# Cross attention on one core: context and its weights split into high and low parts, keys and values made of three rounded products

## The chip, the cores and the metric

The kernel runs on one core of a Trainium2 chip. The metric is the device time of one execution in microseconds. A core has a matrix engine (TensorE, "PE" in the profile, with its weight loads as "PEld"), VectorE ("DVE"), ScalarE ("ACT"), GpSimd ("POOL") and SyncE ("SP"), which here only issues transfers. They work side by side and order each other by semaphores.

## What is computed

The reference is a cross attention of 20 heads of 32 channels with two sets of keys and values: the first 77 rows of the context ("text") and the other 77 ("image"), each with weights of its own. Cut to what matters:

```python
text = encoder_hidden_states[:, :77, :]      # (2, 77, 1024)
ip   = encoder_hidden_states[:, 77:, :]      # (2, 77, 1024)
q    = split_heads(hidden_states @ Wq.T)     # (2, 2048, 640) -> 20 heads of 32
k, v       = split_heads(text @ Wk.T), split_heads(text @ Wv.T)
k_ip, v_ip = split_heads(ip @ Wk_ip.T), split_heads(ip @ Wv_ip.T)
out = merge(attend(q, k, v)) + merge(attend(q, k_ip, v_ip))   # two softmaxes
return out @ Wo.T + bo + hidden_states
```

All arrays are float32.

## The kernel before

There are two stages: a prologue that makes keys and values, and a long loop over 80 units. A unit is one of 16 tiles of 256 query rows and one of 5 groups of 4 heads (128 channels).

**The prologue.** Four products of context and weights are made in this order: keys of text, keys of image, values of text, values of image. Each is `project_ctx` (L692 to 711): for each of the 8 chunks of 128 context channels (k) and each of the 5 groups of output channels (g), one matmul with a 128 x 128 block of the weights as the stationary operand and the context's chunk as the moving one (2 batches x 77 rows = 154 columns), in plain float32, added up in PSUM. That makes 40 matmuls a product, 160 in all. The weights of a product lie in `stage[br]`, 20 KB a partition, br being the branch (text 0, image 1); the context lies in `ctx`. Both arrive in five pieces, `PIECES`, of 1, 1, 2, 2 and 2 chunks, and TensorE waits for a piece (semaphores `ctx_loaded`, `wk_loaded`, `wv_loaded`) ahead of its first chunk. The value weights take the place of the key weights in `stage`, so SyncE (L244 to 256) sends for those of the text branch when the first product is done (`k_acc` at 1) and for those of the image branch when the second is (`k_acc` at 2). The query weights (1.6 MB) and the first tile of x go between the pieces of the text values.

Each engine's program is a list worked off in order. Around the prologue these are:

- ScalarE (L439 to 462): waits for `k_acc`, copies the keys out of PSUM in ten pieces (`keep_keys`), copies the query weights to their rounded high part (`weight_high`, L413), does the same for x (`split_x`), copies its half of the values of text out (`keep_v`), then begins with the first units.
- VectorE: subtracts the high part of the query weights from the raw ones (`weight_low`, L478 to 481), copies the other half of the values out (`keep_v`, L535), then the softmax of the first units.
- TensorE: a few warm-up matmuls (L729), the four products, and within the last of them the query projections of the first two units (`project_q`, 15 matmuls each) and the scores of these units, so that softmax work can start.

The end of the first use of the value banks is a hand-over: TensorE can't begin the fourth product before both halves of the third one's result are copied out (`v_kept`).

**Products of high and low parts.** The query and output projections are already made in another way: each float32 operand is split into a part rounded to the type `F32R` (the ScalarE copy) and the rest (raw less high, the VectorE or GpSimd subtraction, also `F32R`), and the product is the sum of three matmuls in `F32R`: high x high, low x high, high x low (`product_step`, L567 to 572). There the moving operand has 256 columns.

**The loop.** For each unit, TensorE does scores (L595), the query projection two units ahead (L571), the weighing of values (L623, L625), transposes of probabilities (L607, L615) and the output projection of six units before (L571); the other engines do the softmax. The change leaves the loop as it is.

## Time and profile before

| | us |
|---|---|
| time, median of 3 runs (lowest, highest) | 624.54 (622.1, 625.01) |
| the profiled execution's own time | 623.43 |
| its span in the profile | 621.4 |
| TensorE matmul busy, in the span | 599.5 |
| VectorE, ScalarE, GpSimd busy | 417.7, 338.6, 310.1 |

All rows come from one profiled execution. The span begins at its first instruction; times of day in the rows count from there. "Busy" of TensorE is the time with at least one matmul in flight: matmuls are pipelined, so the time from one start to the next (the pace) is shorter than the duration of one record. A pace is therefore read from a run of many records, not from their mean. The chain that ended last is followed back from the last instruction to what released each step; it tells what set the time. Idle time of an engine outside that chain costs nothing.

### The profile page before, as it was taken

The page shows a single profiled execution, that of the slowest core. Times are in us where ns is not written, and L with a number is a line of the kernel's source. Part 1 is how long each engine was busy: PE and PEld are TensorE (multiplying, and loading weights), DVE is VectorE, ACT ScalarE, POOL GpSimd, SP SyncE. Part 2 cuts the span into 40 slices and gives each one's busy share as a digit, 9 for nine tenths or more (in the row PEclk, how much of TensorE's full clock was granted, in tenths as well). Part 3 has the DMA queues.
Part 4 walks back from the last instruction along what each step waited for, and adds up shares of the span by engine and source line. Part 5 has one row for each costly group of instructions (what it writes and reads, how often), then busy time and mean ns, then how long its engine had stood idle before and what let it go on. Part 6 is the DMA issues. An engine that isn't in the chain of part 4 may idle for free.

```text
span 621.4 us, 14491 instructions
## 1 busy us (share of the span) xinstructions
PE 599.5 (96%) x5634; PEld 515.9 (83%) x5634; DVE 417.7 (67%) x496; ACT 338.6 (54%) x674; POOL 310.1 (50%) x341
## 2 busy tenths in 40 slices
PE   8999768999999999999999999999999999999986
PEld 8998557888888888888888888888888888888865
DVE  0035577777777777777777777777777777777761
ACT  0324554565666565656656565655656565565541
POOL 0033544465564746574655557465647555564550
PEclk9999888999999999999999999999999999999999
DMA  8980201112121212121121212121211112111001
GB/s 308 414 333 0 77 2 52 35 44 87 35 86 42 76 39 81 41 76 42 36 82 38 84 38 76 42 84 34 84 38 45 69 42 84 34 45 43 26 28 51
DMA packets 29402, 46.21 MB, mean 74 GB/s; under 512 B 3392, under 2 KB 24512, under 8 KB 29120
## 3 DMA queue, kind: packets, MB, share of 16 engines
q1 hardware_dynamic: 29376, 45.84, 21.5%
q8 instruction: 19, 0.31, 0.2%
q14 instruction: 7, 0.06, 0.0%
HBM read 35.34 MB, written 10.49 MB: 74 GB/s over the span
## 4 chain that ended last, share of the span: by engine, by line
PE 91%; ACT 4%; DVE 3%; DMA 1%; POOL 1%; SPq 0%; issue 0%; DVEq 0%
PE q_ps L571 24%; PE x_ps L571 21%; PE main_ps L607 11%; PE s_ps L595 9%; PE pv_ps L625 7%; PE pv_ps L623 7%; PE s_ps L707 3%; PE pv_ps L615 3%; PE pv_ps L707 2%; PE main_ps L707 1%; DVE row_max L489 1%; ACT probs L363 1%; ACT p_main L368 1%; DMA stage<-wk_in 1%; PE s_ps L658 1%; DVE wo_lo L481 1%
## 5 line engine op out<-in xcount | busy, mean ns | idle before, releaser
L306 POOL TENSOR_TENSOR probs<-probs,row_inv 128x616 f32<-128x616 f32 (+1 forms) x160 | 159.8, 1020 | 239.8 <-DVE row_inv L508 239.8
L489 DVE TENSOR_REDUCE row_max<-s_ps 128x16 f32<-128x1232 f32 x80 | 115.3, 1441 | 75.0 <-PE s_ps L595 75.0
L505 DVE TENSOR_REDUCE row_sum<-probs 128x16 f32<-128x1232 f32 x80 | 114.9, 1436 | 17.5 <-ACT probs L363 17.5
L497 DVE TENSOR_TENSOR probs<-s_ps,row_max 128x616 f32<-128x616 f32 x160 | 120.5, 794 | 2.7
L363 ACT ACTIVATE probs<-probs 128x616 f32<-128x616 f32 x160 | 114.2, 715 | 13.4 <-DVE probs L497 13.4
L358 ACT ACTIVATE q<-q_ps 128x256 f32<-128x256 f32 x80 | 30.6, 383 | 147.1 <-PE q_ps L571 147.1
L607 PE MATMUL main_ps<-ident,probs 128*122 128x128 f32 x640 | 96.6, 274 | 12.5 <-ACT p_main L368 9.1
L368 ACT ACTIVATE p_main<-main_ps 122x512 f32<-122x512 f32 x160 | 94.9, 593 | 15.5 <-PE main_ps L607 15.4
L607 PEld LDWEIGHTS main_ps<-ident,probs 128*122 128x122 f32 x640 | 75.6, 138 | 22.9 <-ACT p_main L368 10.5
L571 PE MATMUL q_ps<-x_hi,wq_hi 128*128 128x256 f32 x400 | 83.0, 306 | 0.0
L571 PE MATMUL x_ps<-attn_hi,wo_hi 128*128 128x256 f32 x375 | 75.2, 298 | 0.0
L571 PE MATMUL q_ps<-x_hi,wq_lo 128*128 128x256 f32 x400 | 74.5, 284 | 0.0
L571 PE MATMUL q_ps<-x_lo,wq_hi 128*128 128x256 f32 x400 | 74.1, 283 | 0.0
L512 DVE TENSOR_TENSOR attn_lo<-pv_ps,attn_hi 128x256 fp32r<-128x256 f32 x80 | 34.0, 425 | 57.5 <-ACT attn_hi L391 57.5
L571 PE MATMUL x_ps<-attn_lo,wo_hi 128*128 128x256 f32 x375 | 69.4, 283 | 0.0
L571 PEld LDWEIGHTS q_ps<-x_hi,wq_hi 128*128 128x128 f32 x400 | 58.6, 191 | 12.9 <-issue 12.6
L571 PE MATMUL x_ps<-attn_hi,wo_lo 128*128 128x256 f32 x375 | 69.1, 282 | 0.0
L297 POOL TENSOR_TENSOR x_lo<-x_raw,x_hi 128x1280 fp32r<-128x1280 f32 x16 | 48.9, 3055 | 37.6 <-ACT x_hi L380 37.6
L595 PE MATMUL s_ps<-keys,q 32*128 32x154 f32 x1280 | 65.7, 320 | 0.0
L386 ACT ACTIVATE y<-x_ps,bo 128x256 f32<-128x256 f32 x74 | 35.0, 473 | 53.9 <-PE x_ps L571 53.9
L571 PEld LDWEIGHTS q_ps<-x_hi,wq_lo 128*128 128x128 f32 x400 | 60.0, 192 | 0.0
L571 PEld LDWEIGHTS q_ps<-x_lo,wq_hi 128*128 128x128 f32 x400 | 59.3, 190 | 0.0
(71 smaller groups left out, 790.5 us busy)
## 6 DMA issues: line engine op xcount, KB each, us to landing
x_raw<-x_in SPq DMA_DIRECT2D x16, 640.0 KB, 3.8
res<-x_in SPq DMA_DIRECT2D x75, 128.0 KB, 2.0
y_out<-res SPq DMA_DIRECT2D x75, 128.0 KB, 1.7
stage<-wk_in SPq DMA_DIRECT2D x6, 640.0 KB, 8.2
stage<-wv_in SPq DMA_DIRECT2D x6, 640.0 KB, 10.7
wq_raw<-wq_in SPq DMA_DIRECT2D x1, 1600.0 KB, 11.2
wo_raw<-wo_in SPq DMA_DIRECT2D x1, 1600.0 KB, 7.4
stage<-wk_in SPq DMA_DIRECT2D x4, 320.0 KB, 5.7
```

What stands on the lines that cost most here:

```text
L297: nc.gpsimd.tensor_tensor(x_lo[:, u.batch], x_raw[:], x_hi[:, u.batch].bitcast(F32), ALU.subtract).then_inc(x_lo_done, 1)
L306: nc.gpsimd.tensor_tensor(rows[:, :, keys], rows[:, :, keys], row_inv[:, u.slot, :, br].unsqueeze(2) .broadcast_to([P, GROUP * SUB, size]) ...
L363: nc.scalar.activation(probs[:, u.slot, heads], probs[:, u.slot, heads], ACT.Exp).then_inc(exp_done, 1)
L368: nc.scalar.activation(p_main[0:MAIN, :, s * P:(s + 1) * P], main_ps[0:MAIN].rearrange("p (j n) -> p j n", j=GROUP), ACT.Copy).then_inc(ma ...
L489: nc.vector.tensor_reduce(row_max[:], by_row(s_ps[:, :, 0:SUB * BLK]), AXIS.X, ALU.max).then_inc(max_done, 1)
L497: nc.vector.tensor_tensor(by_row(probs[:, u.slot, heads].rearrange("p j s n -> p j (s n)")), by_row(s_ps[:, heads, 0:SUB * BLK]), row_max[ ...
L505: nc.vector.tensor_reduce(row_sum[:], by_row(probs[:, u.slot].rearrange("p j s n -> p j (s n)")), AXIS.X, ALU.add).then_inc(sum_done, 1)
L571: return nc.tensor.matmul(out, (lo if kind == 1 else hi)(k), (moving_lo if kind == 2 else moving_hi)(k), start=(n == 0), stop=(n == STEPS_ ...
L595: done = nc.tensor.matmul(s_ps[:, j, s * BLK:(s + 1) * BLK], q[rows_of(j), u.slot, s * P:(s + 1) * P], keys[rows_of(j), u.g, u.batch].rear ...
L607: done = nc.tensor.transpose(main_ps[0:MAIN, j * P:(j + 1) * P], probs[:, u.slot, j, s, 0:MAIN], ident[:])
L623: nc.tensor.matmul(pv_ps[rows_of(j), 0:N], v[:, u.g, u.batch, rows_of(j)], p_main[:, j, :], start=True, stop=False, skip_group_check=True)
L625: nc.tensor.matmul(pv_ps[:, 0:N], v[:, u.g, BATCHES + u.batch, :], p_rest[:], start=False, stop=True, skip_group_check=True).then_inc(pv_r ...
```

## The change

It touches the prologue only.

- New tiles: `stage_lo` and `ctx_lo` lie over `stage` and `ctx` (the low part is written over the raw data), `ctx_hi` is new, and `w_hi` is one buffer for the high parts of a whole product's weights, used by all four products in turn.
- ScalarE copies each piece of the context (keys' products only) and of the weights to its high part (`ctx_high`, `chunk_high`). From the second product on, a piece of `w_hi` may be written only when TensorE has used the same piece of the product before (`w_used`, and for the last piece `k_acc` or `v_acc`). The copies of keys, the split of the query weights and of x and the copy of the values are put between these copies in an order written out by hand.
- VectorE makes the low parts (`ctx_low`, `chunk_low`), with the low part of the query weights between those of the third product.
- TensorE waits for the low parts in place of the transfers, and makes three `F32R` matmuls with 154 moving columns in place of one in float32: 480 in place of 160.

```diff
@@ -144,8 +144,13 @@
         p_rest = sbuf("p_rest", [P, N])
 
         with ExitStack() as before:
-            stage = [sbuf(f"stage{i}", [P, CTX_CHUNKS * C], scope=before) for i in range(BRANCHES)]
-            ctx = sbuf("ctx", [P, BRANCHES, CTX_CHUNKS, BATCHES, KEYS], scope=before)
+            with ExitStack() as raw_before:
+                stage = [sbuf(f"stage{i}", [P, CTX_CHUNKS * C], scope=raw_before) for i in range(BRANCHES)]
+                ctx = sbuf("ctx", [P, BRANCHES, CTX_CHUNKS, BATCHES, KEYS], scope=raw_before)
+            stage_lo = [sbuf(f"stage_lo{i}", [P, CTX_CHUNKS * C], F32R, scope=before) for i in range(BRANCHES)]
+            ctx_lo = sbuf("ctx_lo", [P, BRANCHES, CTX_CHUNKS, BATCHES, KEYS], F32R, scope=before)
+            ctx_hi = sbuf("ctx_hi", [P, BRANCHES, CTX_CHUNKS, BATCHES, KEYS], F32R, scope=before)
+            w_hi = sbuf("w_hi", [P, CTX_CHUNKS, C], F32R, scope=before)
         attn_hi = sbuf("attn_hi", [P, BATCHES, GROUPS, N], F32R)
         attn_lo = sbuf("attn_lo", [P, BATCHES, GROUPS, N], F32R)
         res = sbuf("res", [P, GROUPS, N])
@@ -169,6 +174,9 @@
         wo_hi_done, wo_lo_done = sem("wo_hi_done"), sem("wo_lo_done")
         consts = sem("consts")
         head_rows_done = sem("head_rows_done")
+        ctx_hi_done, ctx_lo_done = sem("ctx_hi_done"), sem("ctx_lo_done")
+        w_hi_done, w_lo_done = sem("w_hi_done"), sem("w_lo_done")
+        w_used = sem("w_used")
         k_acc = sem("k_acc")
         k_done = sem("k_done")
         v_acc = sem("v_acc")
@@ -202,6 +210,17 @@
         v_banks = [pv_ps, main_ps]
         turn_banks = [x_ps, pv_ps, main_ps]
 
+        LAST_PIECE = len(PIECES) - 1
+
+        product_loaded = [*wk_loaded, *wv_loaded]
+        product_acc = [(k_acc, 1), (k_acc, 2), (v_acc, 1), (v_acc, 2)]
+
+        def piece_number(product, n):
+            return product * len(PIECES) + n + 1
+
+        def chunks_of(product, halves):
+            return halves[product % BRANCHES][:].rearrange("p (k c) -> p k c", k=CTX_CHUNKS)
+
         def rows_of(j):
             return slice(j * D, (j + 1) * D)
 
@@ -436,12 +455,40 @@
                 nc.scalar.activation(v[:, g], turn_banks[g % 3][:].rearrange("p (i c) -> p i c", i=VALUES),
                                      ACT.Copy).then_inc(v_done, 1)
 
+            def ctx_high(br, n):
+                first, end = PIECES[n]
+                act.wait_ge(ctx_loaded[br][n], DMA)
+                nc.scalar.activation(ctx_hi[:, br, first:end], ctx[:, br, first:end], ACT.Copy).then_inc(ctx_hi_done, 1)
+
+            def chunk_high(product, n):
+
+                first, end = PIECES[n]
+                act.wait_ge(product_loaded[product][n], DMA)
+                if product > 0 and n < LAST_PIECE:
+                    act.wait_ge(w_used, (product - 1) * LAST_PIECE + n + 1)
+                elif product > 0:
+                    act.wait_ge(*product_acc[product - 1])
+                nc.scalar.activation(w_hi[:, first:end], chunks_of(product, stage)[:, first:end], ACT.Copy).then_inc(w_hi_done, 1)
+
             act.wait_ge(consts, 2)
-            for item in range(K_ITEMS):
+            for br in range(BRANCHES):
+                for n in range(len(PIECES)):
+                    ctx_high(br, n)
+                    chunk_high(br, n)
+            for item in range(GROUPS):
                 keep_keys(item)
+            for n in range(3):
+                chunk_high(2, n)
             weight_high(wq_hi[:], wq_raw[:], wq_loaded, wq_hi_done)
+            for n in (3, 4):
+                chunk_high(2, n)
             split_x(Unit(0, 0))
+            for item in range(GROUPS, K_ITEMS):
+                keep_keys(item)
+            for n in range(LAST_PIECE):
+                chunk_high(3, n)
             keep_v(0)
+            chunk_high(3, LAST_PIECE)
             keep_q(Unit(0, 0))
             for half in range(2):
                 exp(Unit(0, 0), half)
@@ -539,8 +586,32 @@
                                       v_banks[1][:, 0:2 * BATCHES * KEYS].rearrange("p (g b n) -> p g b n", g=2, b=BATCHES)
                                       ).then_inc(v_kept[1], 1)
 
+            def ctx_low(br, n):
+                first, end = PIECES[n]
+                dve.wait_ge(ctx_hi_done, br * len(PIECES) + n + 1)
+                nc.vector.tensor_tensor(ctx_lo[:, br, first:end], ctx[:, br, first:end],
+                                        ctx_hi[:, br, first:end].bitcast(F32), ALU.subtract).then_inc(ctx_lo_done, 1)
+
+            def chunk_low(product, n):
+
+                first, end = PIECES[n]
+                dve.wait_ge(w_hi_done, piece_number(product, n))
+                nc.vector.tensor_tensor(chunks_of(product, stage_lo)[:, first:end], chunks_of(product, stage)[:, first:end],
+                                        w_hi[:, first:end].bitcast(F32), ALU.subtract).then_inc(w_lo_done, 1)
+
+            for br in range(BRANCHES):
+                for n in range(len(PIECES)):
+                    ctx_low(br, n)
+                    chunk_low(br, n)
+            for n in range(3):
+                chunk_low(2, n)
             weight_low(wq_hi[:], wq_raw[:], wq_lo[:], wq_hi_done, 1, wq_lo_done)
+            for n in (3, 4):
+                chunk_low(2, n)
+            for n in range(LAST_PIECE):
+                chunk_low(3, n)
             keep_v(0)
+            chunk_low(3, LAST_PIECE)
             find_max(Unit(0, 0))
             for half in range(2):
                 take_max(Unit(0, 0), half)
@@ -694,21 +765,37 @@
                 if u.fixed and u.number() == OUT_LAG - 1:
                     pe.wait_ge(wo_lo_done, GROUPS)
 
-            def project_ctx(banks, weights_loaded, br, chunks, done_sem):
-
-                w = stage[br][:].rearrange("p (k c) -> p k c", k=CTX_CHUNKS)
+            def project_ctx(banks, product, chunks):
+
+                br = product % BRANCHES
+                w_lo = chunks_of(product, stage_lo)
+                done_sem, _ = product_acc[product]
+
+                def moving(c, k):
+                    return c[:, br, k].rearrange("p b n -> p (b n)")
+
                 for k in chunks:
-                    for n, (first, _) in enumerate(PIECES):
+                    for n, (first, end) in enumerate(PIECES):
                         if k == first:
-                            pe.wait_ge(ctx_loaded[br][n], DMA)
-                            pe.wait_ge(weights_loaded[br][n], DMA)
+                            if product < BRANCHES:
+                                pe.wait_ge(ctx_lo_done, product * len(PIECES) + n + 1)
+                            pe.wait_ge(w_lo_done, piece_number(product, n))
+                        if k < end:
+                            piece, piece_end = n, end
+                            break
                     for g in range(GROUPS):
-
-                        done = nc.tensor.matmul(banks[g % 2][:, group_cols(g)], w[:, k, g * P:(g + 1) * P],
-                                                ctx[:, br, k].rearrange("p b n -> p (b n)"), start=(k == 0 and g < 2),
-                                                stop=(k == CTX_CHUNKS - 1), skip_group_check=True)
+                        cols = slice(g * P, (g + 1) * P)
+                        passes = [(w_hi, moving(ctx_hi, k)), (w_lo, moving(ctx_hi, k)),
+                                  (w_hi, moving(ctx_lo, k))]
+                        for n, (w, c) in enumerate(passes):
+
+                            done = nc.tensor.matmul(banks[g % 2][:, group_cols(g)], w[:, k, cols], c,
+                                                    start=(k == 0 and g < 2 and n == 0),
+                                                    stop=(k == CTX_CHUNKS - 1 and n == PASSES - 1), skip_group_check=True)
                     if k == CTX_CHUNKS - 1:
                         done.then_inc(done_sem, 1)
+                    elif k == piece_end - 1:
+                        done.then_inc(w_used, 1)
 
             def turn_v(g):
 
@@ -728,14 +815,14 @@
             for _ in range(WARM_UP):
                 nc.tensor.matmul(x_ps[:, 0:P], ident[:], ident[:], start=True, stop=True)
             for br in range(BRANCHES):
-                project_ctx(k_banks[br], wk_loaded, br, range(CTX_CHUNKS), k_acc)
-            project_ctx(v_banks, wv_loaded, 0, range(CTX_CHUNKS), v_acc)
+                project_ctx(k_banks[br], br, range(CTX_CHUNKS))
+            project_ctx(v_banks, BRANCHES, range(CTX_CHUNKS))
 
             pe.wait_ge(k_done, K_ITEMS)
             first = Unit(0, 0)
 
             def project_ip_values(first_chunk, end):
-                project_ctx(v_banks, wv_loaded, 1, range(first_chunk, end), v_acc)
+                project_ctx(v_banks, BRANCHES + 1, range(first_chunk, end))
 
             for n in range(2):
                 pe.wait_ge(v_kept[n], 1)
```

## Rows read from the trace of the kernel before

**Rows 1.** The page: busy time by engine, and the chain by engine.

```profile
PE 599.5 (96%) x5634; PEld 515.9 (83%) x5634; DVE 417.7 (67%) x496; ACT 338.6 (54%) x674; POOL 310.1 (50%) x341
PE 91%; ACT 4%; DVE 3%; DMA 1%; POOL 1%; SPq 0%; issue 0%; DVEq 0%
```

**Rows 2.** Chain that ended last, 0 to 75 us: start, length, what.

```profile
8.89 18.57 PE s_ps L707 x140
...
28.50 0.53 PE pv_ps L707 x4
...
37.67 0.28 PE pv_ps L707 x2
37.97 0.57 ACT v_chan L429
38.53 0.12 issue
38.66 0.50 PE pv_ps L707 x2
...
41.51 1.78 PE q_ps L571 x15
...
44.60 0.74 PE s_ps L595 x16
...
53.91 0.57 ACT v_chan L429
...
59.95 0.44 PE main_ps L607 x4
```

**Rows 3.** Lines by form, 0 to 66 us: count, busy us, mean ns.

```profile
L707 PE MATMUL s_ps<-ctx,stage 128*128 128x154 f32 x160 | 22.5, 304 | 0.3 <-DMA stage<-wk_in 0.3
L707 PE MATMUL pv_ps<-ctx,stage 128*128 128x154 f32 x96 | 18.8, 296 | 0.7 <-ACT v_chan L429 0.7
L707 PEld LDWEIGHTS pv_ps<-ctx,stage 128*128 128x128 f32 x96 | 14.7, 190 | 1.1 <-issue 1.1
L707 PE MATMUL main_ps<-ctx,stage 128*128 128x154 f32 x64 | 13.6, 294 | 0.0
L571 PEld LDWEIGHTS q_ps<-x_hi,wq_lo 128*128 128x128 f32 x25 | 3.7, 188 | 0.0
L607 PEld LDWEIGHTS main_ps<-ident,probs 128*122 128x122 f32 x8 | 0.9, 137 | 0.0
```

**Rows 4.** Windows of the prologue: busy by engine, clock, DMA share, GB/s.

```profile
0.00:2.00 2.00, 0.47 (x2) 0.47 (x3) 0.95 (x2) 0.00 (x0) 0.70 (x6) 1.00 0.05 11
2.00:3.00 1.00, 1.00 (x7) 1.00 (x7) 0.25 (x1) 0.00 (x0) 0.00 (x0) 1.00 0.83 136
...
10.00:20.00 10.00, 10.00 (x79) 10.00 (x78) 0.00 (x0) 2.35 (x6) 0.00 (x0) 1.00 1.03 400
20.00:30.00 10.00, 10.00 (x78) 10.00 (x78) 0.00 (x0) 1.54 (x6) 0.00 (x0) 1.00 1.02 420
30.00:37.00 7.00, 7.00 (x56) 7.00 (x55) 3.49 (x1) 3.66 (x2) 3.04 (x1) 1.00 1.03 407
```

**Rows 5.** Timeline of TensorE, 0 to 9 us.

```profile
1.53 3.35 PE L729 MATMUL x_ps<-ident 128*128 128x128 f32 x14 [1.53 <-POOL ident L292]
4.68 3.89 PE L707 MATMUL s_ps<-ctx,stage 128*128 128x154 f32 x20
8.89 0.37 PE L707 MATMUL s_ps<-ctx,stage 128*128 128x154 f32 x1 [0.32 <-DMA stage<-wk_in]
```

**Rows 6.** Waits in 0 to 66 us: total, times, longest.

```profile
DVE wq_lo L481 <- ACT wq_hi L416: 30.2, 1, 30.2
ACT L422 <- PE s_ps L707: 17.1, 1, 17.1
```

**Rows 7.** Weight loads right after the first scores, timeline 45.3 to 45.4 us.

```profile
45.26 0.30 PEld L707 LDWEIGHTS pv_ps<-ctx,stage 128*128 128x128 f32 x2 [0.16 <-issue]
```

**Rows 8.** Timelines of ScalarE and VectorE: the splits that exist.

```profile
29.52 2.87 ACT L416 ACTIVATE wq_hi<-wq_raw 128x3200 fp32r<-128x3200 f32 x1 [0.97 <-DMA wq_raw<-wq_in]
32.61 1.27 ACT L380 ACTIVATE x_hi<-x_raw 128x1280 fp32r<-128x1280 f32 x1 [0.21 <-DMA x_raw<-x_in]
...
32.42 3.49 DVE L481 TENSOR_TENSOR wq_lo<-wq_raw,wq_hi 128x3200 fp32r<-128x3200 f32 x1 [30.17 <-ACT wq_hi L416]
73.60 1.56 DVE L481 TENSOR_TENSOR wo_lo<-wo_raw,wo_hi 128x640 fp32r<-128x640 f32 x2 [3.77 <-ACT wo_hi L416]
```

**Rows 9.** SyncE's issues of transfers, timeline 0 to 66 us.

```profile
0.75 0.38 SPq L240 DMA_DIRECT2D ctx<-ctx_in  x1
...
17.01 1.28 SPq L241 DMA_DIRECT2D stage<-wv_in  x3
18.33 1.37 SPq L247 DMA_DIRECT2D wq_raw<-wq_in  x1
...
27.49 2.23 SPq L241 DMA_DIRECT2D stage<-wv_in  x5
```

**Rows 10.** Windows around the one later stretch at the lower clock.

```profile
65.00:71.80 6.80, 3.18 (x26) 1.99 (x25) 4.08 (x6) 2.69 (x5) 6.73 (x6) 1.00 0.39 127
71.80:75.20 3.40, 3.40 (x27) 2.76 (x26) 1.60 (x3) 2.12 (x4) 1.28 (x2) 0.50 0.27 93
```

## The prediction

> **What bounds the kernel now.** I read the page first: the matrix engine is busy for 96% of the span and its work makes up 91% of the chain that ended last [rows 1]. So TensorE's order of work is the clock of this kernel, and what the change adds to or takes from that order before the long loop shows one to one in the time. The second view is the chain in order of time. Up to 53.9 us it is made of the four products of context and weights (keys and values, of text and of image branch), broken only by the hand-over of the values' banks (0.57 us of ScalarE, and an idle TensorE around it), two query projections of 15 matmuls and one set of scores [rows 2]. The third is the instructions by form: 160 + 96 + 64 records for 160 matmuls, so a plain fp32 product of 128 x 128 by 154 columns is two records; 140 of them in 18.57 us is 132.7 ns a record, and 130 to 131 ns where nothing interferes, thus 262.5 ns a matmul and 42.0 us for all 160 [rows 2, 3]. The fourth is transfers: from 10 to 37 us the DMA engines are at a share of 1.0 and move 400 to 420 GB/s [rows 4]. Yet TensorE stops for a transfer only once, 0.32 us at 8.9 us [rows 5], so transfers are close behind but not the bound. ScalarE and VectorE are nearly empty there: ScalarE waits 17.1 us before its first work and VectorE 30.2 us before the split of the query weights [rows 6].
>
> **The change, part by part.**
>
> *TensorE.* Each of the 160 matmuls becomes three (high by high, low by high, high by low), 480 in all, in the rounded fp32 type. The trace has this type only with 256 moving columns: one record each, 15 in 1.78 us = 119 ns [rows 2]. No row shows it with 154 columns. Bounds: if columns alone set the pace, 154/256 x 119 = 71.4 ns; if 154 columns cost what 154 columns cost in a plain record, 131 ns; if the type gives nothing at 154 columns and each of the three takes both records, 262.5 ns. Break-even against 262.5 ns for three is 87.5 ns, so everything hangs on this number.
>
> I take 112 ns, because of the weight loads. Every one of the 480 matmuls brings a 128 x 128 load of its own (the three alternate between high and low weights, so none can be kept). The load of the rounded type is as long as the plain one, 188 to 190 ns for both, while the load of a transpose of nearly as many columns is 137 ns [rows 3]: the fp32 load is the slow kind. After a gap two fp32 loads start 0.11 us apart (0.30 us for the pair less 0.19 for the last) with no matmul between them to hold the second back [rows 7]. That is a floor of 110 ns under each pair of load and matmul, hidden today under 131 ns of columns, and nearly equal to the 256 columns of the query products (119). With 154 columns the load is what is left. So 112 ns, nearest the load row, with 119 as the end on that side: fewer columns buy almost nothing, and three matmuls take 336 ns in place of 262.5.
>
> [...]
>
> *The start.* Before, TensorE begins the products at 4.68 us and takes the third piece at 8.89 us, at once when it lands [rows 5]. Now a piece must be copied by ScalarE (128 x 1280: 1.27 us, the row of the same shape) and then subtracted by VectorE (3.49 us for 3200 elements a partition, 1.09 ns an element, 1.4 us for 1280) [rows 8]. Third piece: 8.89 + 1.27 + 1.4 + about 0.2 for two more semaphores = 11.8 us. The two pieces before it (30 matmuls, 3.4 us at 112 ns) are ready at about 6.1 us and end before that even at half the pace; half the pace is possible there: the warm-up matmuls of 128 columns take 0.24 us each, later transposes of 128 columns 0.11, so I read the clock as at its lower level in these first microseconds, though the windows print 1.00 [rows 2, 4, 5]. From 11.8 us 450 matmuls remain.
>
> *Do the splits keep up behind that?* Per full piece of two chunks TensorE now takes 30 x 0.112 = 3.4 us, a transfer of 640 KB 1.6 us at 405 GB/s [rows 4], ScalarE 1.27, VectorE 1.4 us. All of them are faster than TensorE, so after the third piece it should not wait. The waits added: ScalarE's copy into the one shared buffer of high parts waits for TensorE's use of the same piece of the product before. Behind it on ScalarE's queue stand the keys' copies, the split of the query weights and x; their users come more than a product later. TensorE reads one piece while the next product's earlier pieces are rewritten, so at 112 ns there are always at least two pieces in hand. The split of the query weights (2.87 + 3.49 us) now stands before pieces 4 and 5 of the text values, and it waits for a transfer that starts later than before (next part). By that part the query weights land at 31.3; 31.3 + 2.9 + 3.5 + 1.4 for the piece itself = 39.1 us, and TensorE wants it four chunks into its third product, at 35.3 + 4 x 1.68 = 42.0. That is cover of about 3 us, which goes if the products get faster.
>
> *The gates of the transfers.* SyncE still waits for the end of the first and second product before it sends the value weights [rows 9]. These ends move from 17.0 to 11.8 + 90 x 0.112 = 21.9 and from 27.5 to 35.3 us. The first transfer of the kernel moves its data about 2 us after its issue (issued at 0.75; 11 GB/s up to 2 us, then 136) [rows 4, 9]. So the queue now runs dry before 24 us; from there 1.31 MB of values land by 27.2 and 1.64 MB of query weights by 31.3 at 405 GB/s. Values of the text branch are wanted at 35.3, those of the image branch land from 38 and are wanted at 49.5 us. The output weights, later by some 5 us, were split first at 73 us [rows 8]. Cost zero; cover 8 us and more.
>
> *After the products* nothing changes: the same query projections, scores and transposes, later by the same amount.
>
> **The sum.** End of the last value product: 11.8 + 450 x 0.112 (50.4) + 0.8 for the bank hand-over (last matmul of the old values to the next start, 37.9 to 38.7) + two query projections 3.6 + scores with their gaps 1.0 = 67.6 us. Before: 53.9 [rows 2]. Difference +13.7 us. The profiled execution took 623.43 us for a span of 621.4; with the difference 637.1. The median of the runs, 624.54, is 1.1 above it, so **638.2 us**. With 110 ns it is +12.8, with 119 ns +16.9 (641.4). A chance of the clock: in the stretch from 71.8 to 75.2 us it is at its lower level after TensorE had been idle for half of the 6.8 us before [rows 10]. A shift or the new gap before the third piece may add or remove one such stretch, 3.4 us at half pace: 1.7 us either way.
>
> **The rivals.**
>
> *One record, columns at the plain price (131 ns).* For it: every row of this kernel with 154 columns and 128 rows stands at 131 ns; against it: those are two-record products, and the query products move 256 columns in less. Sum: 11.8 + 59.0 + 5.4 = 76.2, +22.3, 646.8 us.
>
> *The change doesn't do what it says: the rounded type gives nothing at 154 columns*, two records for each of the three. For it: no row shows the type with anything but 256 columns; against it: nothing in the trace shows a limit either. 450 x 0.2625 = 118.1, end at 135.3, +81.4, about 706 us.
>
> *Columns set the pace, splits late (71 ns).* Product one ends at 11.8 + 6.4 = 18.2, its successor 8.6 later, and the value weights start to move at 20.6, when the keys' 6.5 MB are in. The query weights land at 27.9; the fourth piece of the text values stands behind both halves of their split (27.9 + 2.9 + 3.5 = 34.3, + 1.4 = 35.7), so that product ends 4.3 later at 40.0 and not at 35.4. The copy of the values then stands behind VectorE's fourth piece of the image values, itself copied only when the old piece is used up (42.6); + 120 x 0.071 + 4.6 = 55.8, +1.9, 626.4 us. So even the good pace is given back, and that is within half a per cent of no change.
>
> *Faster:* columns set the pace and the splits are never late. The mechanism is the same 71.4 ns, and its place is the 450 matmuls: 11.8 + 32.1 + 0.8 + 4.6 = 49.3, -4.6, 619.9 us. It decides from a pace below (53.9 - 11.8 - 5.4) / 450 = 82 ns. Against it: the 110 ns between loads, and the queue of the case before.
>
> **How the numbers follow.** Paced by loads, 110 to 119 ns: 0.62. One record at 131 ns: 0.13. Two records: 0.16. Columns with late splits: 0.05. Columns without: 0.02. Something unforeseen that cancels the loss to within half a per cent: 0.02. The prediction is the first case. The range reaches from the case of columns with late splits (626) to the 131 ns case with the clock stretch of 1.7 us and some spread (650); it leaves out the two-record case, the faster one and small tails, together about 0.2. A measurement of this kernel tells 0.5% (3.1 us) from no change: faster 0.02, same 0.07 (late splits and the unforeseen), slower 0.91.
>
> **What would show it.** In the changed profile: 480 records of the context products in place of 320, each 0.11 us after the one before in the long runs (right), 0.07 or 0.13 (a rival), 960 records (the type gives nothing). Weight loads touching end to end through the products. TensorE's first long stretch from about 11.8 us; values' accumulation done at about 67.6 us; in the waits, TensorE on VectorE's low parts only before the first three pieces. The loop behind should take the same time as before, about 568 us from the end of the last value product. The prediction is wrong if the pace at 154 columns is not near the load's, or if TensorE waits for low parts in the middle of a product.

## The result and the profile after

The changed kernel takes 675.88 us (median of 4 executions, 674.72 to 677.43), the kernel before 623.36 us beside it (622.1 to 625.01). The ratio is 1.0839 with a 95% interval of 1.0819 to 1.0859: 52.5 us slower, where 13.7 were forecast, and 26 us above the top of the range.

First the chain in order of time (start, length, what), the view that answers to [rows 2]:

```profile
4.41 0.64 ACT w_hi L471
5.07 0.84 DVE stage_lo L599
6.04 51.45 PE s_ps L792 x240
...
83.13 0.57 ACT v_chan L448
...
90.52 2.55 PE q_ps L642 x15
93.07 0.30 PE pv_ps L792 x3
93.36 0.33 PE main_ps L792 x3
...
94.70 0.73 PE s_ps L666 x16
...
105.79 0.57 ACT v_chan L448
```

The last value product ends at 105.8 us. It ended at 53.9 before, so 51.9 of the 52.5 us are here. The 240 matmuls of the two key products take 51.45 us without a break, 214 ns each; behind the first query projection three of them take 0.33 us, 111 ns each. The same instruction has two prices, and they differ by a factor of 1.9.

The lines by form say the same of the two stretches. From 0 to 110 us, the 80 matmuls of a kind on the keys' banks, then those of 93 to 106 us:

```profile
L792 PE MATMUL s_ps<-ctx_hi,w_hi 128*128 128x154 f32 x80 | 33.3, 416 | 1.1 <-DVE stage_lo L599 1.1
L792 PEld LDWEIGHTS s_ps<-ctx_hi,stage_lo 128*128 128x128 f32 x80 | 26.6, 333 | 0.0
```

```profile
L792 PE MATMUL pv_ps<-ctx_hi,stage_lo 128*128 128x154 f32 x18 | 4.9, 274 | 0.0
L792 PEld LDWEIGHTS pv_ps<-ctx_hi,stage_lo 128*128 128x128 f32 x18 | 3.4, 191 | 0.0
```

A load takes 333 ns in the long stretch and 191 ns at its end, as long there as the loads of [rows 3]. I read these as the two levels of TensorE's clock, the granted clocks that the windows print as 0.50 and 1.00 ([rows 10] has both); the ratio here is 1.7 for the loads and 1.9 for the pace. Windows of the prologue (start and end, length, busy us and instructions of each engine, clock, DMA share, GB/s) show a trap in reading them:

```profile
7.00:30.00 23.00, 23.00 (x110) 23.00 (x109) 12.34 (x16) 10.11 (x15) 0.00 (x0) 1.00 0.58 221
30.00:50.00 20.00, 20.00 (x95) 20.00 (x95) 5.78 (x5) 7.72 (x10) 0.00 (x0) 1.00 0.64 247
50.00:90.00 40.00, 39.23 (x185) 39.05 (x185) 13.33 (x9) 10.26 (x14) 3.06 (x1) 1.00 0.32 124
```

TensorE is busy for nearly all of it and the clock column prints 1.00, yet fewer than 4.8 matmuls start in a microsecond. The column first goes below 1.00 at 122 us in this trace, and at 71 us in that of the kernel before, whose warm-up at 0.24 us a matmul has 1.00 too [rows 4, 5]. Ahead of its first change I don't trust it, and count the matmuls in a window instead. The DMA share, 1.0 before [rows 4], is 0.64 and less, so no transfer is the cause.

The waits show what did go as forecast. In 0 to 110 us TensorE waits for low parts once, before the first piece, and once for the hand-over of the values' banks:

```profile
PE s_ps L792 <- DVE stage_lo L599: 1.1, 1, 1.1
PE pv_ps L792 <- ACT v_chan L448: 0.8, 1, 0.8
```

Behind the prologue nothing changed. The windows from just after the last value product to the end, after and then before:

```profile
107.00:672.80 565.80, 548.11 (x5238) 465.77 (x5238) 406.79 (x486) 327.81 (x655) 304.08 (x334) 0.99 0.17 53
```

```profile
55.10:621.40 566.30, 547.45 (x5238) 465.04 (x5238) 407.03 (x486) 327.76 (x655) 304.19 (x334) 0.99 0.16 53
```

### The profile page after: what moved, and what is told of

It is laid out like the page before. It is cut to its first block, busy times and chain, and to the rows that moved or that the text cites. A ratio compares the mean times of both kernels' runs of the same rounds, so it can differ in the third digit from the quotient of the medians.

```text
span 672.8 us, 14877 instructions
## 1 busy us (share of the span) xinstructions
PE 651.1 (97%) x5794; PEld 567.8 (84%) x5794; DVE 446.6 (66%) x526; ACT 362.0 (54%) x704; POOL 308.4 (46%) x341
## 4 chain that ended last, share of the span: by engine, by line
PE 93%; ACT 3%; DVE 2%; POOL 1%; DMA 0%; issue 0%; DVEq 0%; ACTq 0%
PE q_ps L642 23%; PE x_ps L642 19%; PE main_ps L678 10%; PE s_ps L666 8%; PE s_ps L792 8%; PE pv_ps L696 7%; PE pv_ps L694 6%; PE pv_ps L792 4%; PE main_ps L792 2%; PE pv_ps L686 2%; ACT p_main L387 1%; ACT probs L382 1%; DVE row_max L536 1%; PE s_ps L729 1%; DVE probs L544 0%; DVE wo_lo L528 0%
## 5 line engine op out<-in xcount | busy, mean ns | idle before, releaser
L377 ACT ACTIVATE q<-q_ps 128x256 f32<-128x256 f32 x80 | 30.6, 383 | 151.3 <-PE q_ps L642 151.3
L316 POOL TENSOR_TENSOR x_lo<-x_raw,x_hi 128x1280 fp32r<-128x1280 f32 x16 | 47.2, 2952 | 63.7 <-ACT x_hi L399 63.7
L642 PEld LDWEIGHTS q_ps<-x_hi,wq_hi 128*128 128x128 f32 x400 | 58.8, 192 | 12.9 <-issue 12.6
L405 ACT ACTIVATE y<-x_ps,bo 128x256 f32<-128x256 f32 x74 | 35.0, 473 | 53.9 <-PE x_ps L642 53.9
```

Source lines behind the costliest of these rows:

```text
L316: nc.gpsimd.tensor_tensor(x_lo[:, u.batch], x_raw[:], x_hi[:, u.batch].bitcast(F32), ALU.subtract).then_inc(x_lo_done, 1)
L642: return nc.tensor.matmul(out, (lo if kind == 1 else hi)(k), (moving_lo if kind == 2 else moving_hi)(k), start=(n == 0), stop=(n == STEPS_ ...
```

## The experiments

The theory after this reading, **A**: the stream of 154 columns per 128 x 128 load doesn't lift the clock, though it keeps it once something else has lifted it; here the clock came up within the query projection at 90.5 us, whose matmuls have 256 columns (15 in 2.55 us, 1.78 in [rows 2], and 111 ns a matmul behind it). Rivals: **B**, the stream can't keep it either; **C**, the gap of 1.15 us after the warm-up is the cause; **D**, the rounded type is the cause, whatever its columns; **E**, the splits and waits are the cause.

### A longer warm-up

```diff
-WARM_UP = 7
+WARM_UP = 16
```

> The changed kernel with 16 warm-up matmuls in place of 7, nothing else. In the changed kernel TensorE ran its 420 context matmuls up to 90.5 us at 213 ns each and the last 60 at 112 ns. Theory A (the stream paced by weight loads cannot lift the clock, but holds it once something denser has lifted it): the longer warm-up ends at about 8 us at the full clock, the products run at 112 ns throughout, the last value product ends at about 67 to 69 us and the time is 637 to 641 us. Theory B (the stream cannot hold the clock either, and the fast end of the changed kernel was carried by the query projections in it): the pace falls back to 213 ns within a few us of the start of the products and the time is 665 to 676 us.

One correction to it: 390 of the 480 matmuls, not 420, were at 213 ns. Measured: 634.7, 641.2, 674.2 and 639.3 us; the ratio of the three short ones to the kernel before is 1.0264 (1.0242 to 1.0287). The chain of the profiled one (634.7 us):

```profile
1.53 6.17 PE x_ps L816 x32
7.71 26.91 PE s_ps L792 x240
48.05 0.57 ACT v_chan L448
52.34 1.82 PE q_ps L642 x15
...
66.87 0.57 ACT v_chan L448
```

26.91 / 240 = 112 ns, and the last value product ends at 66.87 us. Nine more matmuls of warm-up give back some 37 us. B falls as it was written, since the stream keeps the clock for 45 us, from 7.7 us to the first query projection. But one execution of the four, 674.2 us, took as long as the changed kernel, with a mean granted clock of 0.933: the clock is kept, and can be lost.

### The splits and waits with one plain matmul

```diff
-passes = [(w_hi, moving(ctx_hi, k)), (w_lo, moving(ctx_hi, k)),
-          (w_hi, moving(ctx_lo, k))]
+passes = [(w_hi, moving(ctx_hi, k))]
...
-    ... w[:, k, cols], c,
+    ... w[:, k, cols].bitcast(F32), c.bitcast(F32),
```

> The changed kernel with all splits, buffers and waits, but only one matmul in plain float32 (high weights by high context, read as float32) in place of the three; the two products with low parts are left out. It prices the splits and waits alone. My working: the start of the third piece moves from 8.9 to 11.8 us and nothing else, +2.7 us, 626 us. Rival (splits late behind faster products, or the hand-written order costs more): over 630 us, with waits of TensorE on low parts in the middle of a product. If the clock of the changed kernel were kept low by the new gap after the warm-up, this kernel would run its plain matmuls at half pace too: +40 us, about 665 us.

Measured: 633.23 us (631.04 to 638.96), ratio 1.0148 (1.013 to 1.0166). That is 9.5 us over the 623.77 us of the kernel before on the same chip, not 2.7, and not 40. So E isn't the cause of the 52 us, yet my price of the splits was too low for this kernel. Windows and first instructions after a wait in the profiled execution (638.96 us, the slowest of five):

```profile
12.00:18.60 6.60, 5.74 (x22) 5.77 (x23) 6.21 (x9) 5.06 (x9) 0.00 (x0) 0.50 1.04 399
18.60:42.00 23.40, 20.87 (x159) 20.64 (x158) 13.27 (x12) 14.37 (x17) 0.00 (x0) 1.00 0.80 312
```

```profile
12.86 21.38 PE L791 MATMUL s_ps<-ctx_hi,w_hi 128*128 128x154 f32 x140 [3.38 <-DVE stage_lo L599]
42.66 0.88 PE L791 MATMUL pv_ps<-ctx_hi,w_hi 128*128 128x154 f32 x2 [3.19 <-DVE stage_lo L599]
51.63 0.50 PE L791 MATMUL pv_ps<-ctx_hi,w_hi 128*128 128x154 f32 x2 [1.90 <-DVE v_chan L585]
```

It waits for the third piece, then for the fourth piece of the text values behind the query weights' split (the cover that I had said goes if the products get faster), then for VectorE's copy of the values; and the clock falls in or just after each of the three (the printed clock goes from 1.00 to 0.50 at about 11.8, 42.5 and 52.7 us). The first two times the plain stream is back at the full clock 5.7 and 3.2 us after it goes on, the third time the query projection is under way by then; the rounded stream of the changed kernel did not come back in 84 us. In this execution the three waits are 8.5 us; 46 matmul records behind them start some 0.257 us apart and not 0.131, an estimated 6 us more. So a good part of what the splits cost here is again the clock.

### More columns for the same loads

```diff
 def moving(c, k):
-    return c[:, br, k].rearrange("p b n -> p (b n)")
+    return c[:, br, k].rearrange("p b n -> p (b n)")[:, 0:P].unsqueeze(1).broadcast_to([P, 2, P])
...
-nc.tensor.matmul(banks[g % 2][:, group_cols(g)], ...
+nc.tensor.matmul(wide(banks[g % 2], g), ...          # 256 columns of the bank
```

> The changed kernel with 256 moving columns in each of the 480 matmuls (128 columns of the chunk read twice, written to 256 columns of the bank): two thirds more columns, same loads, keys and values are then not those of the reference. At the lower clock 256 columns take 213 ns, as long as the load, so the stream is as long there as with 154. If density of columns lifts the clock (theory A and B): the clock rises within the first 10 us or so, pace 119 ns from then on, time about 641 us, 30 us faster than the changed kernel although it does more. If the rounded type with one record per matmul, or the gap after the warm-up, kept the clock low: the pace stays at 213 ns or more and the time at 676 us or above.

Measured: 640.99 us (two executions, 640.63 and 641.34), ratio 1.0276 (1.0256 to 1.0297). With two thirds more columns than the changed kernel, the same warm-up and nearly the same gap after it (1.11 us, 1.15 there), it is 35 us faster. Windows:

```profile
6.00:9.40 3.40, 3.40 (x16) 3.40 (x17) 1.30 (x3) 1.56 (x3) 0.00 (x0) 1.00 0.97 345
9.40:40.00 30.60, 30.11 (x249) 29.92 (x249) 18.98 (x19) 19.23 (x26) 0.00 (x0) 1.00 0.82 315
```

16 matmuls in 3.4 us (213 ns each, as in the changed kernel), then 249 in 30.6 (123 ns): the clock came up at 9.4 us. It stayed up over a wait of 0.49 us ahead of the third piece. C and D both fall here: the type is the rounded one, and the gap is there.

### Fewer columns in the plain type

```diff
-nc.tensor.matmul(banks[g % 2][:, group_cols(g)], w[:, k, ...],
-                 ctx[:, br, k].rearrange("p b n -> p (b n)"), ...
+nc.tensor.matmul(half_cols(banks[g % 2], g, k % 2), w[:, k, ...],
+                 ctx[:, br, k, k % 2], ...            # 77 columns
```

> The kernel before, plain float32, with 77 moving columns in place of 154 (one batch per chunk, alternating; half of the products left out). It makes the plain type paced by its loads. If the load paces and such a stream cannot lift the clock: 320 records at 213 ns, the products take 68 us instead of 42 and the time is about 648 us, slower with half the work (if the query projections lift it at the end, some 640). If the low clock comes from the rounded type only: the clock rises at about 7 us as before, 320 records at 110 ns, 35 us, and the time is about 617 us. [...]

Measured: 642.77 us (642.38, 643.15), ratio 1.0305 (1.0284 to 1.0325). The kernel *before*, with half of its context columns taken out, is 19 us slower. Lines by form from 8 to 60 us:

```profile
L711 PE MATMUL s_ps<-ctx,stage 128*128 128x77 f32 x146 | 31.6, 418 | 0.1
L711 PEld LDWEIGHTS s_ps<-ctx,stage 128*128 128x128 f32 x145 | 31.1, 333 | 0.2 <-issue 0.2
```

Loads of 333 ns again, and 140 records in 30.12 us of the chain, 215 ns each. It is the changed kernel's illness in the other type, which is the second leg against D. In each of the two types the run with the fewer columns to a load stayed at the lower level (154 rounded, 77 plain) and the run with the more came up before 10 us (256 rounded at 9.4 us; 154 plain at about 7 us, where a window of 1 us goes from 6 records to 9 in the kernel before).

### Closing the gap only

```diff
-WARM_UP = 7
+WARM_UP = 9
```

> The changed kernel with 9 warm-up matmuls in place of 7: they end at about 5.9 us, when the first low parts are ready, so that TensorE has no gap before the products, but no time at the full clock either. If the gap of 1.15 us after the warm-up was what kept the clock low: it rises at about 7 us as in the kernel before and the time is 635 to 641 us. If the products themselves can't lift it: 213 ns a matmul up to the first query projection as in the changed kernel, 675 us.

Measured: 674.51 us (674.29, 674.73), ratio 1.082 (1.0791 to 1.085), the time forecast for A. But the trace tells more than either theory did:

```profile
6.35 0.28 PE L792 MATMUL s_ps<-ctx_lo,w_hi 128*128 128x154 f32 x1
...
9.79 0.28 PE L792 MATMUL s_ps<-ctx_lo,w_hi 128*128 128x154 f32 x1
12.62 0.47 PE L792 MATMUL s_ps<-ctx_hi,w_hi 128*128 128x154 f32 x1 [2.56 <-DVE stage_lo L599]
12.88 0.42 PE L792 MATMUL s_ps<-ctx_hi,stage_lo 128*128 128x154 f32 x1
```

```profile
14.00:90.00 76.00, 75.23 (x353) 75.05 (x353) 27.57 (x25) 24.36 (x34) 3.04 (x1) 0.50 0.43 164
```

In this execution the clock was up when the products began (0.28 us a matmul, 0.11 apart). Being fast, TensorE had used up the first two pieces at 9.9 us and waited 2.56 us for the third. Behind that wait it was at the lower level and stayed there for 80 us of work that only the hand-over of 0.8 us breaks. The window prints 0.50 at 4.6 matmuls a microsecond, where those of the changed kernel print 1.00 at 4.8; here the change itself is in the trace, between 12 and 13 us. So the fast start hurt itself: against the 640.0 us of the next experiment, the loss behind one wait of 2.6 us cost some 35 us. The prologues in the other traces agree: waits of 3.2 and 3.4 us (one plain matmul) and 4.7 us (half loads) left the clock down, those of up to 0.98 us (77 columns with 16 warm-up matmuls) left it up. In between it went either way: after one of 1.90 us it fell (one plain matmul), after one of 1.98 us it stayed (half loads). One of the four executions of the changed kernel itself (676.6 us) prints a mean granted clock of 0.929, like the 0.933 here, where the others print 0.989 and 0.990; it may have had the clock at the start and lost it in the same way, but it left no trace.

### A warm-up that reaches past that wait

```diff
-WARM_UP = 7
+WARM_UP = 24
```

> The changed kernel with 24 warm-up matmuls. With 16, three executions took 634.7 to 641.2 us and one 674.2, whose mean granted clock of 0.933 says that the clock rose in the warm-up and was lost for most of the products. 24 end some 1.8 us later, so the products start near 9.7 us and there is no wait ahead of the third piece (ready at 11.8). If the short wait at the third piece is what loses the clock: all executions at 636 to 642 us. If the stream of 154 columns holds the clock only by luck: again some near 675 us. The extra warm-up itself costs about 1 us of start.

Measured: six executions from 637.6 to 644.0 us, two of them above the 642 expected, median 640.02, ratio 1.028 (1.025 to 1.0311). The products start at 9.7 us and no wait is left in front of the third piece:

```profile
1.53 8.19 PE x_ps L816 x48
9.72 26.77 PE s_ps L792 x240
...
68.74 0.57 ACT v_chan L448
```

Six of six keep the clock (mean granted clocks of 0.981 to 0.991), against three of four with 16. That fits the wait as the cause of the loss in the one execution of 674.2 us, but that execution left no trace, and six are few; it is likely, not shown.

### A burst in the middle

```diff
 for br in range(BRANCHES):
+    if br == 1:
+        for _ in range(20):
+            nc.tensor.matmul(x_ps[:, 0:P], ident[:], ident[:], start=True, stop=True)
     project_ctx(k_banks[br], br, range(CTX_CHUNKS))
```

> The changed kernel with its 7 warm-up matmuls, and 20 matmuls of identity by identity in plain float32 (40 records, result not used) between the first and the second product. My theory: the stream paced by loads does not lift the clock but keeps it once it is up. Then product one runs at 213 ns up to about 31.6 us, the burst lifts the clock within its first 4 to 7 us and ends after some 6 to 8 us, and products two to four run at 112 ns: last value product at about 86 to 90 us, time 652 to 659 us, some 20 us faster than the changed kernel for 40 records more. If the start of the kernel decides (or the clock falls again): the time is that of the changed kernel plus the burst, 680 to 684 us.

Measured: 652.26 us (651.91, 652.62), ratio 1.0467 (1.0436 to 1.0497). The chain:

```profile
6.14 25.85 PE s_ps L792 x120
31.99 5.54 PE x_ps L820 x40
37.54 13.37 PE s_ps L792 x120
...
83.15 0.57 ACT v_chan L448
```

120 matmuls at 215 ns, 5.5 us of matmuls whose result nobody reads, 120 at 111 ns. The 40 useless records make the changed kernel 23.6 us faster. So what lifts the clock and what keeps it are separate things here, and it was lifted in the middle as well as at the start: the window from 33 to 34 us has 6 records, that from 34 to 35 has 10.

### What the 112 ns are

```diff
-cols = slice(g * P, (g + 1) * P)
+rows = slice(0, P if k == 0 else 64)
+cols = slice(g * P + rows.start, g * P + rows.stop)
...
-nc.tensor.matmul(banks[g % 2][:, group_cols(g)], ...
+nc.tensor.matmul(banks[g % 2][rows, group_cols(g)], ...   # and WARM_UP = 24
```

> The changed kernel with 24 warm-up matmuls and, from the second chunk of each product on, weight blocks of 64 columns instead of 128 (half of the output channels gets its first chunk only, so keys and values are not those of the reference). The moving operand keeps its 154 columns. It asks what the 112 ns at the full clock are. If they are the 128-column load: 420 of the 480 matmuls go at 65 to 80 ns, and the products end several us earlier than with 24 warm-up matmuls and full loads (68.7 us in that trace), time 625 to 633 us, limited by the splits of the query weights. If it is a fixed price of a matmul in the rounded type with so few columns: 112 ns a matmul still, 638 to 640 us.

Measured: 630.65 us (629.4, 631.89), ratio 1.012 (1.0072 to 1.0168). The chain has the third to last pieces of the first key product as

```profile
11.90 6.77 PE s_ps L793 x90
```

75 ns a matmul with loads of 64 columns and the same 154 moving columns. So the 112 ns at the full clock come from the 128-column load: with whole loads behind the same 24 warm-up matmuls, 240 matmuls took 26.77 us. From there on the splits set the pace (`stage_lo` of VectorE and the query weights' transfer lead that chain), so the total says little more.

The same trace holds one more test of A. In the values of text TensorE waits 4.7 us for a low part, and the clock is down when it goes on. Its first matmul behind the wait, and windows before and after 43 us:

```profile
37.65 0.39 PE L793 MATMUL pv_ps<-ctx_hi,w_hi 128*64 128x154 f32 x1 [4.71 <-DVE stage_lo L599]
```

```profile
37.65:42.60 4.95, 4.92 (x36) 4.69 (x37) 4.95 (x3) 3.36 (x6) 2.73 (x1) 0.50 0.55 190
43.00:44.40 1.40, 1.40 (x22) 1.40 (x21) 1.40 (x2) 0.13 (x1) 0.00 (x0) 1.00 1.15 470
```

The matmuls start 0.129 us apart up to 42.7 us and 0.074 us apart from 43 us on: with the load halved, this stream of 154 rounded columns came back to the full clock by itself, 5.1 us after it went on. With the whole load it did not in 80 us. So the 154 columns didn't keep the clock down by themselves; they did so together with the whole load (213 ns a matmul for 80 us).

### Half the columns at the full clock

```diff
-WARM_UP = 7
+WARM_UP = 16          # on top of the 77 columns in the plain type
```

> The kernel before with 77 of 154 moving columns (half of the products left out) and 16 warm-up matmuls. With 7, its clock rose only at 65 us and the time was 642.8 us. It asks what the load costs at the full clock with hardly any columns beside it. Load floor of 110 ns a record: products of 35 us from about 9 us on, end some 3 us earlier than in the kernel before, 619 to 621 us if the clock holds. [...] If the clock is lost again soon after the warm-up (38% fewer columns per load than in the rounded products): 640 us.

Measured: eight executions from 619.5 to 627.8 us, median 625.28, ratio 1.0025 (0.9997 to 1.0052). Lines by form, 8 to 50 us:

```profile
L711 PE MATMUL s_ps<-ctx,stage 128*128 128x77 f32 x153 | 17.4, 275 | 0.0
L711 PEld LDWEIGHTS s_ps<-ctx,stage 128*128 128x128 f32 x151 | 17.0, 192 | 0.1
```

17.4 us for 153 records is 114 ns with 77 columns, near the 112 ns of the rounded stream with 154 and the same loads, so I take it for the load again. The values' end moved to 50.7 us in the profiled execution (619.5 us), 3 us early as the load theory has it, though 1.8 us of waits for value weights are in it. That is the 619 to 621 us expected, but only two of the eight executions are in that range; the median is 2 us slower than the kernel before; mean granted clocks of 0.978 to 0.985 in six of the eight, against 0.991 and 0.992 in the two fastest, say that most had further stretches at the lower level. Half of the columns of the context products are gone and the median gains nothing.

### Fillers in the kernel before

```diff
+early = u.fixed and u.number() < OUT_LAG
+if early and u.number() == 2:
+    fill(12)
 turn_main(last, 0)
+if early and u.number() > 2:
+    fill(7)
 if chunk.exists():
```

> The kernel before with fillers: 12 matmuls of identity by identity ahead of the probabilities' transposes in unit 2 and 7 between the two transposes of units 3 to 5, where TensorE waits for ScalarE and GpSimd; their result is not used. In the kernel before the clock is at its lower level for three stretches of 3.4 us (71.8, 88.8, 99.1 us) behind such waits. If idle time there loses the clock: these stretches go, and up to 3 us with them, 620.5 to 623 us. If the stretches cost nothing because ScalarE and VectorE set the pace there: 623.5 us; if the fillers stand in the way: 625 us and more.

Measured: 622.41 us (621.85 to 624.34, twelve executions), ratio 0.9992 (0.9981 to 1.0004): no difference clear of the noise. The kernel before has three stretches at the lower level, the one of [rows 10] and these:

```profile
88.80:92.30 3.50, 3.50 (x28) 2.86 (x27) 1.16 (x3) 2.70 (x4) 2.58 (x3) 0.51 0.01 2
99.10:102.50 3.40, 3.40 (x19) 3.08 (x22) 2.85 (x3) 0.19 (x1) 3.40 (x4) 0.50 0.01 2
```

The same three windows with the fillers, and two rows of the chain between the first two:

```profile
71.80:75.20 3.40, 3.40 (x41) 2.89 (x42) 1.50 (x3) 2.22 (x5) 1.41 (x3) 1.00 0.28 98
88.80:92.30 3.50, 3.50 (x28) 2.86 (x27) 1.21 (x3) 2.70 (x4) 2.49 (x3) 0.53 0.01 2
99.10:102.50 3.40, 3.40 (x30) 2.75 (x31) 2.95 (x3) 1.35 (x3) 3.40 (x4) 1.00 0.01 2
```

```profile
81.84 2.33 DVE wo_lo L481 x2
84.16 1.36 DVE row_max L489
```

Two of the three stretches are gone, and by the interval at most 1.2 us with them; had TensorE set the pace there, up to half of their 6.8 us would have gone. Between the first units the chain leads through ScalarE and VectorE for much of the time, with the output weights' splits on their queues, so TensorE's clock is worth less there than in the prologue. No variant tried beats the kernel before by more than the noise.

## Why the prediction was wrong

- **Bound and place: right.** All of the loss lies in TensorE's products before the loop (51.9 of 52.5 us), and the loop takes what it took.
- **The choice of 112 ns: right as a price at the full clock.** 112 ns in three traces, against the ends 71.4, 131 and 262.5. The reason given, that the 128 x 128 load sets it, is confirmed by the half loads (75 ns) and by the half columns (114 ns). One support for it was weak: the shorter load of the transposes (137 ns for 122 columns, 188 to 190 for 128) stands as `f32` in its row too [rows 3], so the row doesn't show that the type makes a load slow.
- **The step that failed: "450 x 0.112".** It took the clock of the kernel before for given. From the third piece on that kernel's prologue runs at the full clock; I carried that over to another stream of matmuls. Measured, 390 of 480 matmuls cost 213 ns. From the third piece on these are 360 x (0.213 - 0.112) = 36.4 us; the third piece is begun 0.6 us later than the 11.8 us of the sum (30 matmuls at 213 ns from 6.04 us), and the first query projection takes 2.55 instead of 1.8 us. Together 37.8 us; the products ended at 105.8 instead of 67.6, 38.2 us late.
- **The clock stood in the prediction as 1.7 us either way.** I looked at it as a matter of gaps (a stretch after idling, [rows 10]) and priced one stretch. The low level at the very start was even read off the warm-up [rows 5], without the question what would end it. No rival had the products themselves at the lower level. My own bounds could have made me ask: columns alone would take an estimated 71 ns of each 112 (154/256 of the 119 ns of the query products [rows 2]). I used that for the sum and not for the clock. In the kernel before columns set the pace here (131 ns a record, over an estimated 110 ns for the load [rows 7]), and its clock came up at about 7 us, while this same start, the warm-up of 14 records from 1.53 us on, left the changed kernel at the lower level; that difference I did not name.
- **Start of the products: right.** First low parts at 5.9 us, TensorE's start at 6.04 us. The 0.2 us for two semaphores in the sum named no row; the chain above has 0.02 us from ScalarE to VectorE and 0.13 us on to TensorE. In the three traces of the rounded products where TensorE waited for the third piece, it began it at 11.9 us (256 columns, half loads) and 12.6 us (9 warm-up matmuls), 11.8 forecast; with 16 it was ready by 11.0. One sentence there was wrong in its sum: at half the pace the first 30 matmuls do not end before 11.8 us but at 6.1 + 30 x 0.213 = 12.5, which is the 0.6 us above.
- **Splits keep up: right for three matmuls, and too cheap for fewer.** There is no wait of TensorE on low parts after the first at 213 ns, and none at 112 ns either with 16 or 24 warm-up matmuls. With one plain matmul of 262.5 ns in place of the three (336) the splits cost 9.5 us and not 2.7, through the two queues that the rival with late splits had named and through the clock behind the waits.
- **The rivals.** None was the case. The two-record rival would have given 706 us by twice the records; the records are single, and most of them start 213 ns apart. The forecast of 638.2 us, which has the clock up, is near what the kernel does with 24 warm-up matmuls, 640.0 us.

## What to carry to other kernels

Before an edit shortens the moving operand or the time per matmul, ask what sets the pace afterwards: if it is the weight load, further columns saved may be worth nothing (77 in place of 154 in the kernel before, with 16 warm-up matmuls, took 625.28 us against 623.24), and the clock itself comes into question: here such matmuls started 213 ns apart and not 112 for 84 us while the profile showed a fully busy engine. Check it by counting matmuls in a window, not by the busy share. Nine more matmuls of warm-up ahead of the stretch were worth 37 us in three executions of four; and a faster engine may run into a wait that costs it the clock, as with 9 warm-up matmuls (2.56 us).

## What was not expected of the hardware

- A stream of 128 x 128 loads with 154 columns each in the rounded type stayed at the lower clock (213 ns a matmul) for 84 us, from 6.0 to 90.5 us with one break of 0.8 us, and so did the plain type with 77 columns (loads of 333 ns) for more than 50 us. With 256 columns on the same loads the clock was up at 9.4 us, and with 154 columns on half the load it came back in 5.1 us.
- The same stream kept the full clock once it had it: some 45 us at 112 ns a matmul up to the first query projection after 16 warm-up matmuls, and likewise after 24, or after 5.5 us of plain matmuls in the middle.
- One wait of 2.56 us was enough to lose it, for 80 us; one of 1.98 us in another trace was not.
- Rounded matmuls of 154 columns with a load of 128 columns each started 112 ns apart at the full clock and 213 ns apart at the lower one; with loads of 64 columns it was 75 and 129 ns.
